# Softmax sums from three tiles, q/k loads issued in pairs, and inverse sums spread by TensorE

## What is computed

```python
h = layernorm(x) * (1 + scale) + shift
q, k, v = (h @ Wqkv + bqkv)             # 16 heads of 32, length 2048, batch 2
attn = softmax(einsum('blhd,bmhd->bhlm', q, k) * 32 ** -0.5)
out = einsum('bhlm,bmhd->blhd', attn, v)
x = x + gate * (out @ Wproj + bproj)
h = layernorm(x) * (1 + scale) + shift
x = x + gate * (gelu(h @ W1 + b1) @ W2 + b2)
```

## Time and profile before

| | |
|---|---|
| Median of 3 runs | 3552.14 us (3538.53 to 3553.55) |
| The profiled execution | 3559.65 us, span 3557.9 us |
| PE busy | 3332.5 us, 94% of the span |
| DVE busy | 2007.6 us, 56% |
| POOL busy | 1574.2 us, 44% |
| ACT busy | 1545.4 us, 43% |
| Mean granted TensorE clock | 0.953 of full speed |
| Attention | about 883 to 2643 us of the span |
| Projection | 2643 to 2834 us |
| MLP | 2834 us to the end |

### The profile page before, as it was taken

How to read it: one execution, slowest core, us unless ns; L and a number is a source line. 1 busy time by engine, 2 the same in 40 slices (tenths; PEclk the granted TensorE clock), 3 DMA queues, 4 the chain that set the end, 5 groups by cost and what they waited for, 6 DMA issues and landing times. The chain is left out here.

```text
span 3557.9 us, 45561 instructions
## 1 busy us (share of the span) xinstructions
PE 3332.5 (94%) x17052; PEld 2232.7 (63%) x17052; DVE 2007.6 (56%) x3432; ACT 1545.4 (43%) x2790; POOL 1574.2 (44%) x589
## 2 busy tenths in 40 slices
PE   7989996999999999999999999999977699999999
PEld 6478885777455555555555555555435478888887
DVE  1278884443877778777777777777624232222222
ACT  0011113443266666666666666666643342222221
POOL 1033331000278778778777777777865200000000
PEclk9899997999699999999999999999988799999999
DMA  4222323444557768766766766766656531111100
GB/s 152 85 76 92 93 92 136 173 162 153 139 133 164 169 144 187 169 147 157 170 158 152 180 149 144 170 158 151 161 143 230 198 120 39 39 39 39 39 33 24
DMA packets 201105, 459.05 MB, mean 129 GB/s; under 512 B 62027, under 2 KB 83787, under 8 KB 170190
## 3 DMA queue, kind: packets, MB, share of 16 engines
q1 hardware_dynamic: 142254, 262.44, 22.4%
q0 software_dynamic: 18432, 134.23, 18.5%
q10 hardware_dynamic: 40224, 59.78, 6.7%
HBM read 165.71 MB, written 88.34 MB: 71 GB/s over the span
## 5 line engine op out<-in xcount | busy, mean ns | idle before, releaser
L1249 DVE TENSOR_REDUCE att_mx<-att_pM 128x1 f32<-128x512 f32 x2048 | 1251.9, 682 | 323.3 <-PE att_pM L1307 321.9
L1234 ACT ACTIVATE att_prob<-att_pS 128x512 f32<-128x512 f32 x2048 | 1048.0, 619 | 471.1 <-PE att_pS L1354 468.3
L1175 POOL TENSOR_TENSOR att_acc<-att_acc,att_prob 128x2048 f32<-128x2048 f32 x224 | 1038.8, 4637 | 220.9 <-ACT att_prob L1234 210.1
L1307 PE MATMUL att_pM<-att_ks,att_qs 96*128 96x512 f32 x2048 | 845.4, 421 | 48.2 <-DMA att_ks<-qk_d 48.0
L1354 PE MATMUL att_pS<-att_qs,att_ks 98*128 98x512 f32 x2048 | 850.4, 417 | 2.7 <-ACT att_prob L1234 2.1
L1354 PEld LDWEIGHTS att_pS<-att_qs,att_ks 98*128 98x128 f32 x2048 | 388.8, 190 | 344.2 <-issue 216.1
L1322 PE MATMUL att_pO<-att_prob,att_V 128*32 128x512 f32 x4096 | 512.7, 620 | 0.0
L1307 PEld LDWEIGHTS att_pM<-att_ks,att_qs 96*128 96x128 f32 x2048 | 402.6, 197 | 158.8 <-DMA att_ks<-qk_d 54.5
L1807 DVE TENSOR_TENSOR mlp_us<-mlp_tu,mlp_us 128x512 fp32r<-128x512 f32 x128 | 89.7, 701 | 536.8 <-ACT mlp_us L1780 536.8
L1850 PE MATMUL mlp_pu<-mlp_hs,mlp_W 128*128 128x512 f32 x1536 | 371.7, 391 | 19.8 <-DVE mlp_W L1799 19.5
L1869 PE MATMUL mlp_pa<-mlp_W,mlp_us 128*128 128x512 f32 x1536 | 368.8, 389 | 0.0
(11 more groups left out here) (200 smaller groups left out, 2957.2 us busy)
## 6 DMA issues: line engine op xcount, KB each, us to landing
att_gathered<-att_prob POOLq DMA_DIRECT2D x128, 1024.0 KB, 8.2
att_gathered<-att_prob SPq DMA_DIRECT2D x64, 1024.0 KB, 7.1
qk_d<-qkv_qs SPq DMA_DIRECT2D x64, 512.0 KB, 2.7
att_qs<-qk_d ACTq DMA_DIRECT2D x42, 512.0 KB, 5.1
att_ks<-qk_d ACTq DMA_DIRECT2D x42, 512.0 KB, 10.3
gat_xT<-in_xT SPq DMA_DIRECT2D x32, 256.0 KB, 3.1
gat_xrow<-in_x SPq DMA_DIRECT2D x32, 256.0 KB, 2.8
x_d<-gat_x SPq DMA_DIRECT2D x32, 256.0 KB, 2.1
```

Of the source, the lines that this page charges most:

```text
L1175: nc.gpsimd.tensor_tensor(acc[half][:], old[:], new[:], ALU.add).then_inc(added, 1)
L1234: nc.scalar.activation(prob[step % PR][:, c, :], pS[at % 3][:], ACT.Exp, scale=SCALE).then_inc(exp_done, 1)
L1249: nc.vector.tensor_reduce(mx[:, q // 4, q % 4:q % 4 + 1], bank(at)[:], AX.X, ALU.max).then_inc(m_read, 1)
L1307: nc.tensor.matmul(bank(at)[:], qs[k][0:KD, h, (half * 8 + t) * P:(half * 8 + t + 1) * P], ks[k][0:KD, h, mc * 512:(mc + 1) * 512], start= ...
```

## The change

1. In the attention, POOL issues one more accumulating transfer at the end of each half: it waits for both chains and adds `gathered[1]` onto `gathered[0]`. `finish` then sums three tiles instead of four, and waits for this transfer (`merged`) where it waited for the chains.
2. `LOADS` goes from `[1, 2, 3, 5, 6, 7]` to `[1, 1, 2, 2, 3, 3]`.
3. `invert` makes three small DVE instructions of one, and stores the inverse sums as a high and a low part in `z_d` (now 2 x 16 rows).
4. In the projection, 32 rows of inverse sums are loaded by one transfer, and PE spreads them over 128 partitions by a product with a 0/1 matrix (`inverse`, into a bank `pz`; one product for each row tile of the chunk before). DVE multiplies them in, one product of 128 x 512 at a time, behind the residual add of the chunk before. `high` and `low` work on 128 x 512 pieces, and `high(i + 2)` stands behind the four `ht` in ACT's `body(i)`. `pT` has two banks instead of three.

```diff
-        LOADS = [1, 2, 3, 5, 6, 7]
+        LOADS = [1, 1, 2, 2, 3, 3]
...
                         if ADDED[i] in SENT_BEHIND:
                             send(n, *SENT_BEHIND[ADDED[i]])
+                    for i in range(2):
+                        pool.wait_ge(sent[i], (n + 1) * 32)
+                    nc.gpsimd.dma_start(gathered[0][:], gathered[1][:], accum_op=ALU.add).then_inc(merged, 16)
...
-                if step in LOADS:
-                    load_part(act, g + 1, LOADS.index(step))
+                for i in range(6):
+                    if step == LOADS[i]:
+                        load_part(act, g + 1, i)
...
-                if n >= 1:
+                nc.vector.reciprocal(rec[:], packed[:]).then_inc(rec_ready, 1)
+                if n >= 1:
                     dve.wait_ge(z_kept, 32 * n)
-                nc.vector.reciprocal(packed[:], packed[:]).then_inc(inverted, 1)
+                dve.wait_ge(rec_ready, n + 1)
+                nc.vector.tensor_copy(inv[:, 0, :], rec[:]).then_inc(inv_hi, 1)
+                dve.wait_ge(inv_hi, n + 1)
+                nc.vector.tensor_tensor(inv[:, 1, :], rec[:], inv[:, 0, :], ALU.subtract).then_inc(inverted, 1)
...
-                for i in range(2):
-                    pe.wait_ge(sent[i], (n + 1) * 32)
-                    sums(pS[at % 3], gathered[i], False, False)
+                pe.wait_ge(merged, (n + 1) * 16)
+                sums(pS[at % 3], gathered[0], False, False)
...
-    for c in range(DC):
-        sp.dma_start(zr[:, c, :], io["z_d"][c * HPC:(c + 1) * HPC, at].unsqueeze(1).to_broadcast([HPC, HD, 512])).then_inc(z_loaded, 16)
+    sp.dma_start(raw(zt[:]), io["z_d"].rearrange("w h n -> (w h) n")[:, at]).then_inc(z_loaded, 16)
...
-                act.wait_ge(o_scaled, DC + i)
-                if at_least(i, 2):
-                    act.wait_ge(p_done, i * 4 - 4)
-                nc.scalar.activation(os_[s][:, 0], of[s][:], ACT.Identity).then_inc(o_hi, 1)
+                for c in range(DC):
+                    act.wait_ge(o_scaled, i * DC + c + 1)
+                    if c == 0 and i >= 2:
+                        act.wait_ge(p_done, i * 4 - 4)
+                    nc.scalar.activation(os_[s][:, 0, c, :], of[s][:, c, :], ACT.Identity).then_inc(o_hi, 1)
...
-                    if c == 0 and before(i, NCH - 2):
-                        high(i + 2, s)
...
+                if before(i, NCH - 2):
+                    high(i + 2, s)
...
+                    if i + 1 < NCH:
+                        scale(i + 1, 1 - s, nt, pz)
...
+                            if nt == 0 and n == 2:
+                                pe.wait_ge(o_lo, i * DC + c + 1)
...
+                    if i + 1 < NCH:
+                        inverse(i + 1, 1 - s, nt, pz)
...
-                    if n >= 3:
-                        pe.wait_ge(h_ready, n - 2)
+                    if n >= 2:
+                        pe.wait_ge(h_ready, n - 1)
```

More of the change, by code:

```diff
@@ L961, in attention_phase @@
         zs, oc = m.sb("zs", [P, 512]), m.sb("oc", [P, 512])
-        packed = m.sb("packed", [P, 16])
+        packed, rec = m.sb("packed", [P, 16]), m.sb("rec", [P, 16])
+        inv = m.sb("inv", [P, 2, 16], F32R)
         pS = [m.ps(f"pS{i}") for i in range(3)]
@@ L1105, in keep_inverted @@
                 for h in range(2):
-                    sp.dma_start(z_v[g // 2, h, g % 2, half], packed[h * 64:(h + 1) * 64, :]).then_inc(z_kept, 16)
+                    sp.dma_start(z_v[g // 2, h, g % 2, half], raw(inv[h * 64:(h + 1) * 64])).then_inc(z_kept, 16)
             load_head(sp, 0)
@@ L1118, in _ @@
             sp.dma_start(keep["p_bp"][:], io["rows"][6:7, :].to_broadcast([P, D])).then_inc(weights_early, 16)
+            sp.dma_start(keep["p_heads"][:], io["heads"]).then_inc(weights_early, 16)
             for n in range(2 * NG):
@@ L1408, in proj_phase @@
         ones2 = m.sb("ones2", [2, P], F32R)
-        zr = [keep["p_zr"], m.sb("zr1", [P, DC, 512])]
+        zt = [keep["p_zt"], m.sb("zt1", [2 * H, 512], F32R)]
+        heads = m.sb("heads", [2 * H, DC, P], F32R)
         os_ = [m.sb(f"os{i}", [P, 2, DC, 512], F32R) for i in range(2)]
@@ L1417, in proj_phase @@
         rstd, tmp, shift = m.sb("rstd", [P, 4]), m.sb("tmp", [P, 8]), m.sb("shift", [P, 4])
-        pT = [m.ps(f"pT{i}") for i in range(3)]
+        pT = [m.ps(f"pT{i}") for i in range(2)]
+        pz = m.ps("pz")
         pr = m.ps("pr", [P, 16])
@@ L1562, in _, with scale @@
         def _(dve):
+            def scale(i, s, c, factor):
+                if c == 0 and i >= 1:
+                    dve.wait_ge(o_loaded[s], (i + s) // 2 * 16)
+                dve.wait_ge(z_done, i * DC + c + 1)
+                nc.vector.tensor_tensor(of[s][:, c, :], of[s][:, c, :], factor[:], ALU.mult).then_inc(o_scaled, 1)
+            nc.vector.tensor_copy(heads[:].rearrange("p c n -> p (c n)"), keep["p_heads"][:]).then_inc(heads_ready, 1)
+            for c in range(DC):
+                scale(0, 0, c, pp[c])
             for c in range(DC):
@@ L1611, in _, with inverse @@
         def _(pe):
+            def inverse(i, s, c, out):
+                if c == 0 and i >= 1:
+                    pe.wait_ge(z_loaded[s], (i + s) // 2 * 16)
+                if i >= 2 or c and i == 1:
+                    pe.wait_ge(o_scaled, i * DC + c)
+                nc.tensor.matmul(out[:], heads[:, c, :], zt[s][:], start=True, stop=True).then_inc(z_done, 1)
             def first():
+                pe.wait_ge(heads_ready, 1)
+                for c in range(DC):
+                    inverse(0, 0, c, pp[c])
                 for n, (k, w) in enumerate(PASSES):
@@ L1619, in first @@
                                 pe.wait_ge(w_hi, c + 1)
+                            if n == 0 and c == 0:
+                                pe.wait_ge(o_scaled, nt + 1)
                             if nt == 0 and n == 1:
@@ L1630, in first @@
                             nc.tensor.matmul(pp[nt][:], ones2[:], bias2[:, 0, :], start=False, stop=True).then_inc(p_done, 1)
+                            inverse(1, 1, nt, pz)
             def project(i, s, b):
-                pe.wait_ge(o_lo, DC + i)
                 if b:
@@ L1905, in build @@
             keep["p_of"] = e.sb("of", [P, DC, 512])
-            keep["p_zr"] = e.sb("zr", [P, DC, 512])
+            keep["p_zt"] = e.sb("zt", [2 * H, 512], F32R)
+            keep["p_heads"] = e.sb("heads", [2 * H, D])
             if upto > 2:
@@ L1937, in layouts @@
         "cols": cols, "rows": rows, "wl": wl,
+        "heads": np.tile(np.repeat(np.eye(H, dtype=np.float32), HD, axis=1), (2, 1)),
         "ident": np.eye(P, dtype=np.float32), "floor4": np.array([[0], [0], [1], [1]], np.float32),
```

54 lines of the change are left out of this document (24 added, 30 removed).

## The result

The changed kernel takes **3645.27 us** (median of 4 runs, 3643.25 to 3647.9) against 3552.85 of the kernel before in the same session: a ratio of 1.0254, 95% interval 1.0217 to 1.0292, 92 us slower. The forecast was 3605, the range 3500 to 3655. So the side is right and the time is in the range, but the forecast is 40 us short, and the reason for most of these 40 is a term that the prediction had at nothing.

The account below looks back on a forecast made before the run. PE, busy 94% of the span, was taken to bound the kernel. Terms -26.7 - 77.0 + 133 + 9 + 15 = +53 on the median of 3552.14 gave a forecast of 3605 us, range 3500 to 3655.

Parts of the forecast that it names:

- load waits and their low clock: Attention, step 10: paired loads remove PE's waits for K and the low clock behind them, -77.0 us.
- new transfer with the tile saved: At finish: one tile less, -26.7 us; stalls in 14 halves with loads, +133; the last finish, +9.
- inversion: Attention, DVE: small instructions hidden by four banks of slack before PE waits, at no cost.
- projection: After attention: a new chain makes chunks 22 to 25 us, +15 us in all, bounds -10 and +28.
- the 50.10 of the prediction: Attention: time in us of a half without loads, read from the distance of finishes in the earlier trace.
- The stall of 7 us: At finish in 14 halves with loads: PE waits 7 us for the new transfer, plus 2.5 for low clock.
- the ends named: New transfer beside loads: landing +13 to +15 (stall 5 to 7 us), or at latest +17.9 (stall 9.7).
- The figure of 6 us: New transfer beside loads: q0 starts about 6 us late, as the earlier trace showed behind large packets.
- The rival of fair turns from the start: New transfer: q0 shares with the loads at once, stall 1.5 to 3 us, total 3518 us; chance 0.22.
- starvation to the end: Rival: q0 starts only when q10 is empty, with projection at its worst, 3661 us; no separate chance given.
- the forecast's own case: New transfer at finish: stall of 5 to 10 us, total given as 3545 to 3660 us; chance 0.68.
- the cover: Inversion: DVE's four banks of slack before PE waits; without them 32 x 0.5 = 16 us.

Follow-up runs that it names:

- g3: The whole changed kernel with the three inversion instructions at a later step (INVERT = 12 instead of 9); 3691.67 us, ratio 1.0404.
- e4: The kernel before with the paired loads alone (LOADS = [1, 1, 2, 2, 3, 3]); 3481.86 us, ratio 0.9819.
- e2: The changed kernel without the new transfer, finish summing four tiles again; 3538.35 us, ratio 0.9978.
- e3: The kernel before plus the new transfer alone, with loads, inversion and projection as before; 3610.05 us, ratio 1.019.
- f1: The changed kernel with all six loads behind the new transfer's issue (LOADS = [3, 3, 4, 4, 5, 5]); 3611.73 us, ratio 1.0148.
- f2: e2 with the inversion as one DVE instruction again, the low part left out; 3489.04 us, ratio 0.9798.
- g2: e2 with the three inversion instructions at a later step (INVERT = 11 instead of 9); 3521.67 us, ratio 0.993.
- g1: e2 with the three inversion instructions at a later step (INVERT = 12 instead of 9); 3682.07 us, ratio 1.0377.
- e1: The changed kernel with the inversion's copy replaced by a second reciprocal that writes the high part; 3638.24 us, ratio 1.0266.
- f4: The kernel before with paired loads and the new transfer in even halves alone, inversion and projection as before; 3475.43 us, ratio 0.9763.

## Why the prediction was right, and where it was not

The traces and runs above give each term of the sum. Each is a difference between two kernels, and the last two are told apart by the stretch in which they lie. The transfer is taken with the new inversion in place, the inversion without the transfer; g3 shows that the two can cover each other, so another order could split the sum otherwise.

| term | predicted | measured |
|---|---|---|
| load waits and their low clock | -77.0 | -71 (e4 against before: -70.0 from 1 to 29, -0.9 at the ends); -65 by the medians of that session |
| new transfer with the tile saved | -26.7 + 133 + 9 = +115 | +107 (changed against e2) |
| inversion | 0 | +48 (e2 against e4) |
| projection | +15 | +10 (e2 against e4) |
| sum | +53 | +94 (the medians: +92) |

**The load waits** went as said; e4's halves are 50.66 and 50.06 us (medians), and the 50.10 of the prediction holds within half a us. The profiled execution of the kernel before was one of its slower ones, so a term read from it is a little large.

**The new transfer** was right in place and mechanism, and near in size. The stall of 7 us was 6.97, the low clock stands behind it, the even halves wait for nothing, and the landing at +17.5 in half 5 is within the ends named. That the stall is met so closely is in part luck, for both of its ends came more than a us later than said: the transfer lands at +16.4 on average, where +13 to +15 was said, and PE comes at +9.45, not at +8.15. The whole cost of an odd half is 8.8 us rather than 9.5: 98.2 us up to half 29, plus 29 tiles of 0.86 us, over 14. From half 29 on it cost 9.1 us net of the last tiles, near the 9 predicted. The figure of 6 us that the stall rested on was right by luck of the case, however: the earlier trace rows had given it as a lag, and it goes with the loads in front, four here, two in e3 (3.4 us) and none in f1 (1.45 us). The rival of fair turns from the start falls, and so does starvation to the end, since q0 gets two thirds of the engines from 1277 on while q10 still has loads to move. By the section "Queues, rings and completion order" of "DMA: Bandwidth & Descriptors" in the Trainium skill the engines would take turns. Between q0 and q10 the rows of three kernels don't agree with it at the start: what came first moves alone, and only then do the two share. The premise of that rival, that a stall under 2 us leaves the clock alone, is borne out at `finish`: behind f1's ten waits of up to 1.78 us the granted clock stays at 1.00. At step 10 it isn't: in the kernel before the clock fell to 0.50 with a wait of 1.71 us. Two slips stand in the working: the lower end of the forecast's own case is 3552 - 17 = 3535, not 3545; and loads that are through at about 1276 are through at +11.6, not +12.4. Neither moved the forecast.

**The inversion is the step that failed.** The prediction had "two small DVE instructions (under 0.5 us with their waits) per half, on DVE, which has four banks of slack": nothing, and 16 us if the cover were gone. Both halves of that are wrong. The instructions are small, but one of them is held until POOL's addition ends, 1.73 us at the median. And DVE has no four banks of slack: in the timelines its eight reductions take 4.87 us of each 5.80 that PE needs for two steps, so it catches up by 0.93 us in two steps at most. An estimate of the slack: PE fills a bank every 0.47 us and DVE empties one every 0.61 (4.87 / 8), so eight of them use up 1.1 us of the 1.9 (4 x 0.47) that four banks give, before any hold; a hold of 1.73 us is then more than what is left, and PE follows at DVE's pace. In the changed kernel the halves without a stall (from an odd to an even `finish`) take 51.8 us, where 49.2 was said; the low clock behind the stall is part of that. f2, g2, e2 and g1 give the line: no held instruction, and holds of 1.23, 1.73 and 4.06 us, cost 0, 1.05, 1.61 and 6.5 us a half, the last with the low clock. (No run has the three instructions without a hold; what the two more cost by themselves, about 0.4 us of DVE, is not told apart.) The rule was to be had: the Trainium skill, "SBUF — State Buffer", section "Who interferes with whom", says that DVE and GpSimd share a pair of ports, that copies in their two-port form and instructions with two inputs in SBUF need it, and that whoever comes second is blocked for the whole of the other's instruction. All of e1, f2 and g1 agree: copy and subtraction held, reciprocal never. Their ends agree as well, 0.03 to 0.04 us behind the end of an addition. And its price could have been read from the trace of before: 0.35 us behind the start of the one reciprocal, where the copy now begins, an addition of POOL is under way in 20 of the 32 halves, mostly with 1.7 us still to go.

**The projection** came out 5 us better than its term, within its bounds, with a chunk at 22.4 us on average (157.0 / 7) where 22 to 25 were said. But the wait named for it, for POOL's `low`, is 2.1 us in all; it is ACT's `high` that PE waits for, 16.7 us.

So the total was short by 40 us: +48 that was missed, less 8 and 5 us by which two terms were too dear, and 6 too much gain from the loads. The time lies in the range because the range was made wide for the transfer, up to 3655, and not because the range allowed for this; the 16 us named for the inversion are a third of what it cost.

## What to carry to other kernels

A transfer on the software queue that something waits for is better issued ahead of the large loads than behind them: in these runs its delay grew with the loads in front of it. But then look at what stands behind them in turn, as SP's copies in f1. Before instructions are added on DVE, look at what POOL does at that time, not at how small they are, and at DVE's idle time per period of the loop rather than at the depth of its buffers. And a part whose price differs from half to half can be used in the cheap ones alone: f4 keeps the saved tile where it costs nothing, and the paired loads, and drops the rest.

## What the runs showed of the hardware that was not expected

- Between the software queue q0 and ACT's hardware queue q10, with large packets on both, the one that came first starts first: q0 got going 6.1 us behind its issue with four loads of 512 KB in front, 3.4 us with two and 1.45 us with none, and in this last case loads issued 2.8 us behind it moved nothing for 4 us. Once both had begun they shared the engines.
- A DVE copy of 128 x 16 (float32 to fp32r, 0.17 us at its fastest) and a subtraction of two tiles in SBUF take until 0.03 to 0.04 us behind the end of POOL's addition, up to 4.58 us; reciprocals of the same size take 0.24 us throughout.
- A pause moved to a gap of another engine misses it when the move shifts the gap: g1 aimed at 2.9 us of idle POOL and hit the start of an addition in most halves (median hold 4.06 us).
